# A Householder tridiagonalisation on one core: the next column from the reflected product, with the reflection's factor computed ahead of the product

## The reference

```python
L = jnp.diag(deg) - A
L_norm = d_inv_sqrt[:, None] * L * d_inv_sqrt[None, :]
_, U = jnp.linalg.eigh(L_norm)
agg = jnp.einsum('mn,bnd->bmd', U.T, features)
h = jax.nn.relu(agg @ W1 + b1)
out = h @ W2 + b2
return jnp.einsum('nm,bmd->bnd', U, out)
```

## Time and profile before

| | |
|---|---|
| median of 3 runs | 7619.89 us (7603.49 to 7624.76) |
| profiled execution | 7623.76 us, span 7622.0 us |
| mean granted TensorE clock | 0.811 |
| busy in the span: PE, DVE, ACT, POOL | 65%, 58%, 20%, 11% |
| the tridiagonal stage | 42 to 1437 us |

### The profile page before, as it was taken

How to read it: one execution, slowest core, us unless ns; L and a number is a source line. 1 busy time by engine, 2 the same in 40 slices (tenths; PEclk the granted TensorE clock), 3 DMA queues, 4 the chain that set the end, 5 groups by cost and what they waited for, 6 DMA issues and landing times. The chain is left out here.

```text
span 7622.0 us, 81119 instructions
## 1 busy us (share of the span) xinstructions
PE 4954.3 (65%) x22112; PEld 3479.5 (46%) x22112; DVE 4404.4 (58%) x17933; ACT 1555.7 (20%) x3409; POOL 852.4 (11%) x653
## 2 busy tenths in 40 slices
PE   5666544332003799740079967777697997977999
PEld 5666433210002577520069933333376443646676
DVE  5555666798995333348988866666633223343332
ACT  1111111243001244420000000000043532442333
POOL 0000000001000000000000068888400000000000
PEclk9999999975556799865555578888798997888799
DMA  0000000000000000010000000000000000000000
GB/s 24 1 1 1 1 1 1 1 1 1 1 1 1 12 0 0 2 12 21 0 0 0 0 4 4 4 4 4 3 0 13 0 0 7 0 3 12 1 0 22
DMA packets 72449, 30.60 MB, mean 4 GB/s; under 512 B 46714, under 2 KB 67860, under 8 KB 71956
## 3 DMA queue, kind: packets, MB, share of 16 engines
q1 hardware_dynamic: 52756, 23.65, 1.4%
q0 software_dynamic: 19456, 4.40, 0.9%
HBM read 22.89 MB, written 5.11 MB: 4 GB/s over the span
## 5 line engine op out<-in xcount | busy, mean ns | idle before, releaser
L1274 PE MATMUL l1f_ga_acc<-l1f_gas_prod,l1f_gas_ohl 128*128 128x512 f32 (+1 forms) x1824 | 778.8, 580 | 261.8 <-DVE l1f_gas_prod L1233 174.2
L1161 PE MATMUL l1f_gap_hist<-l1f_gap_ohh,l1f_gap_ohl 128*128 128x64 bf16 x4096 | 539.9, 308 | 361.4 <-DVE l1f_gap_ohh L1145 360.6
L1161 PEld LDWEIGHTS l1f_gap_hist<-l1f_gap_ohh,l1f_gap_ohl 128*128 128x128 bf16 x4096 | 492.8, 149 | 408.4 <-DVE l1f_gap_ohh L1145 400.7
L1274 PEld LDWEIGHTS l1f_ga_acc<-l1f_gas_prod,l1f_gas_ohl 128*128 128x128 f32 x1824 | 359.0, 208 | 681.7 <-issue 425.1
L1249 POOL DMA_INDIRECT l1f_gas_rs<-l1f_ga_table_s,l1f_gas_sidx x304 | 405.6, 1334 | 1016.0 <-DVE l1f_gas_didx L1205 923.6
L1683 PE MATMUL l0g_tri_dots<-l0g_tri_Z 128*128 128x7 f32 (+31 forms) x762 | 208.1, 394 | 462.2 <-DVE l0g_tri_Z L1850 448.5
L1233 DVE TENSOR_TENSOR l1f_gas_prod<-l1f_gas_ohh,l1f_gas_msg 128x1280 f32<-128x1280 f32 x304 | 454.2, 1494 | 10.4
L1249 POOL DMA_INDIRECT l1f_gas_rd<-l1f_ga_table_d,l1f_gas_didx x304 | 416.7, 1371 | 101.5 <-issue 101.5
L1260 ACT ACTIVATE l1f_gas_ex<-l1f_gas_ex 128x32 f32<-128x32 f32 x38 | 8.7, 229 | 2003.8 <-DVEq L1214 1896.2
L1683 PEld LDWEIGHTS l0g_tri_dots<-l0g_tri_Z 128*128 128x128 f32 x762 | 181.4, 318 | 479.6 <-DVE l0g_tri_Z L1848 462.5
L1143 DVE TENSOR_TENSOR l1f_gap_ohl<-l1f_gap_rep,l1f_gae_dlow 128x2048 bf16<-128x2048 bf16 x256 | 314.0, 1226 | 73.1 <-PE l1f_gap_hist L1161 72.6
(11 more groups left out here) (842 smaller groups left out, 10054.4 us busy)
## 6 DMA issues: line engine op xcount, KB each, us to landing
l1f_gas_rs<-l1f_ga_table_s,l1f_gas_sidx POOLq DMA_INDIRECT x304
l1f_gas_rd<-l1f_ga_table_d,l1f_gas_didx POOLq DMA_INDIRECT x304
out_dram<-top_x SPq DMA_DIRECT2D x2, 2048.0 KB, 12.2
l1f_gae_src<-in_L_ffn_edge_index_dram SPq DMA_DIRECT2D x1, 2048.0 KB, 7.3
l1f_gae_dst<-in_L_ffn_edge_index_dram SPq DMA_DIRECT2D x1, 2048.0 KB, 11.8
l2f_w<-in_L_ffn_expert_w_dram SPq DMA_DIRECT2D x3, 384.0 KB
l0f_l0f_W<-in_L_ffn_W_dram SPq DMA_DIRECT2D x1, 1024.0 KB
l1f_l1f_W<-in_L_ffn_W_dram SPq DMA_DIRECT2D x2, 512.0 KB
```

Of the source, the lines that this page charges most:

```text
L1161: last = nc.tensor.matmul(hist[:, :], ohl[:, j, :, c], ohh[:, j, :, c], start=False, stop=False)
L1274: last = nc.tensor.matmul(acc[:, c0 * T:c1 * T], ohl[:, c % 2, :], prod[:, c % 2, c0:c1, :].rearrange("p c t -> p (c t)"), start=False, st ...
```

## The change

The new column is written as (A x) and v alone: base = ya[0] * KV (+ a term for a vanishing column) and x' = vm * late[0] + base, where KV and vm = v * knk now carry the sign and the factor. `nk` is 1 / (root * ax + ns), with ns the squared norm, instead of the clamped sum t2, t3; a column whose squared norm is under 1e-30 gets a flag in ZF, and the flag also replaces the clamp when the vectors are kept. The whole block from ns to vm stands ahead of `ya[0]`; `late[1]` is used for KK only. The copies into VV move from ACT to DVE (`keep_vectors`). TensorE's wait for `w_set` comes after the wait for `applied` and still ahead of every matmul of the step. Its late matmuls wait for `ya_set` and `v_set`, which the instructions themselves raise.

```diff
                     pe.wait_ge(x_set, i + 1)
-                    pe.wait_ge(w_set, i)
                     if J == 0 and i > 0:
                         pe.wait_ge(applied, strip_of(i))
+                    pe.wait_ge(w_set, i)
...
-                    pe.wait_ge(late_in, i + 1)
+                    pe.wait_ge(ya_set, i + 1)
+                    pe.wait_ge(v_set, i + 1)
...
                     act.wait_ge(nk_set, i + 1)
+                    nc.scalar.activation(w["nkh"], w["nk"], ACT.Square, scale=0.5 ** 0.5).then_inc(act_step, 1)
+                    act.wait_ge(y_set, i + 1)
                     nc.scalar.activation(yn[:, h0:], y[:, h0:], ACT.Copy, scale=w["nk"]).then_inc(act_step, 1)
-                    nc.scalar.activation(w["nkh"], w["nk"], ACT.Square, scale=0.5 ** 0.5).then_inc(act_step, 1)
...
+                def keep_vectors(i, k, b):
+                    n = i + 1 - k * STRIP
+                    link(ts(moved[:, 0:n], ZF[:, k * STRIP:i + 1], -1.0, 1.0, ALU.mult, ALU.add))
+                    for h, top in ((0, min(n, P - 1 - k * STRIP)), (1, n)):
+                        if top > 0:
+                            link.free(tt(VV[:, h, k * STRIP:k * STRIP + top], Z[:, b, h, 1:2 * top:2], moved[:, 0:top], ALU.mult))
+                    dve.wait_ge(dve_step, link.n)
+                def current_times_x(i, J, h0, r, corr_at):
+                    dve.wait_ge(prod_done, i + 1)
+                    if J > 0:
+                        dve.wait_ge(dve_step, corr_at)
+                        ins = tt(ya[:, h0:, r, 0], prod[:, h0:HALF], corr[:, h0:], ALU.add)
+                    else:
+                        ins = nc.vector.tensor_copy(ya[:, h0:, r, 0], prod[:, h0:HALF])
+                    ins.then_inc(ya_set, 1)
...
+                    link.free(ts(ZF[:, at], dots[:, 0:1], 1e-30, None, ALU.is_lt))
                     dve.wait_ge(own_done, i + 1)
                     link.free(ts(w["sgn"], own[:, 0:1], 0.0, 2.0, ALU.is_ge, ALU.mult))
-                    link.free(ts(w["al2"], own[:, 0:1], 2.0, None, ALU.mult))
...
+                    link.free(stt(w["ax"], w["sgn"], -1.0, own[:, 0:1], ALU.add, ALU.mult))
+                    link.free(stt(w["ns"], ZF[:, at], 1e30, dots[:, 0:1], ALU.mult, ALU.add))
+                    link.free(stt(NB[:, at], w["sgn"], -1.0, w["root"], ALU.add, ALU.mult))
+                    dve.wait_ge(dve_step, ns_at)
+                    link.free(ts(w["den"], w["root"], w["ax"], w["ns"], ALU.mult, ALU.add))
+                    dve.wait_ge(dve_step, nb_at)
+                    stt(v, eye[:, h0:, r], NB[:, at], x, ALU.mult, ALU.add).then_inc(v_set, 1)
                     link.free(tt(V1[:, at], own[:, 0:1], NB[:, at], ALU.add))
+                    dve.wait_ge(dve_step, den_at)
                     if i > 0:
                         dve.wait_ge(act_step, 2 * i)
-                    link(nc.vector.reciprocal(w["nk"], w["t3"]))
+                    nc.vector.reciprocal(w["nk"], w["den"]).then_inc(nk_set, 1)
+                    link.free(stt(still[:, h0:], ya[:, h0:, r, 1], ZF[:, at], below[:, h0:, r], ALU.mult, ALU.mult))
+                    dve.wait_ge(nk_set, i + 1)
+                    dve.wait_ge(dve_step, v1_at)
+                    link.free(stt(KV[:, at], w["nk"], -1.0, V1[:, at], ALU.mult, ALU.mult))
+                    dve.wait_ge(dve_step, kv_at)
+                    link.free(stt(w["knk"], KV[:, at], -1.0, w["nk"], ALU.mult, ALU.mult))
+                    dve.wait_ge(dve_step, link.n)
+                    dve.wait_ge(v_set, i + 1)
+                    link.free(stt(vm[:, h0:], v, w["knk"], below[:, h0:, r], ALU.mult, ALU.mult))
+                    current_times_x(i, J, h0, r, corr_at)
+                    dve.wait_ge(ya_set, i + 1)
+                    stt(y[:, h0:], ya[:, h0:, r, 1], NB[:, at], ya[:, h0:, r, 0], ALU.mult, ALU.add).then_inc(y_set, 1)
+                    dve.wait_ge(dve_step, kv_at)
+                    link.free(stt(base[:, h0:], ya[:, h0:, r, 0], KV[:, at], below[:, h0:, r], ALU.mult, ALU.mult))
+                    dve.wait_ge(dve_step, base_at)
+                    link.free(tt(base[:, h0:], base[:, h0:], still[:, h0:], ALU.add))
                     dve.wait_ge(dve_step, link.n)
                     dve.wait_ge(late_done, i + 1)
+                    stt(Z[:, nb_next, h0:, 0], vm[:, h0:], late[:, 0:1], base[:, h0:], ALU.mult, ALU.add).then_inc(x_set, 1)
                     link.free(tt(w["c1"], late[:, 1:2], NB[:, at], ALU.mult))
+                    dve.wait_ge(dve_step, link.n)
                     dve.wait_ge(act_step, 2 * (i + 1))
                     link.free(ts(KK[:, at], late[:, 0:1], w["c1"], w["nkh"], ALU.add, ALU.mult))
-                    stt(Z[:, nb_next, h0:, 0], vnm[:, h0:], w["g"], base[:, h0:], ALU.mult, ALU.add).then_inc(x_set, 1)
+                    dve.wait_ge(dve_step, link.n)
+                    stt(wv, v, KK[:, at], yn[:, h0:], ALU.mult, ALU.subtract).then_inc(w_set, 1)
```

More of the change, by code:

```diff
@@ L1629, in tridiagonalise @@
         base = s.sb("base", [P, HALF])
-        vnm = s.sb("vnm", [P, HALF])
+        still = s.sb("still", [P, HALF])
+        vm = s.sb("vm", [P, HALF])
         NB = s.sb("NB", [P, N])
@@ L1635, in tridiagonalise @@
         VA = s.sb("VA", [P, N])
+        ZF = s.sb("ZF", [P, N])
+        moved = s.sb("moved", [P, STRIP])
         pick = s.sb("pick", [P, HALF, N])
-        names = ["sgn", "al2", "root", "t1", "t2", "t3", "nk", "nkh", "kb", "c1", "g1", "g"]
+        names = ["sgn", "ax", "ns", "root", "den", "nk", "nkh", "knk", "c1"]
         row = s.sb("row", [P, len(names)])
@@ L1647, in tridiagonalise @@
         diag_row = s.ps("diag_row", [P, N])
[L1648 to L1652, removed]
+        (masks, zeroed, init, dve_step, act_step, x_set, w_set, dots_done, own_done, prod_done, root_done, ya_set, v_set, nk_set,
+         y_set, late_done, va_kept, swapped, turned_done, turned_kept, rank_done, applied, picked, diag_done) = s.sems(
+            "masks", "zeroed", "init", "dve_step", "act_step", "x_set", "w_set", "dots_done", "own_done", "prod_done", "root_done",
+            "ya_set", "v_set", "nk_set", "y_set", "late_done", "va_kept", "swapped", "turned_done", "turned_kept", "rank_done",
+            "applied", "picked", "diag_done")
         def halves(i):
@@ L1685, in _ @@
                     last.then_inc(dots_done, 1)
-                    nc.tensor.matmul(own[:, 0:1 + 2 * J], eye[:, h1, r:r + 1].to_broadcast([P, P]), Z[:, b, h1, 0:1 + 2 * J],
-                                     start=True, stop=True).then_inc(own_done, 1)
+                    last = nc.tensor.matmul(own[:, 0:1 + 2 * J], eye[:, h1, r:r + 1].to_broadcast([P, P]), Z[:, b, h1, 0:1 + 2 * J],
+                                            start=True, stop=True)
+                    last.then_inc(own_done, 1)
                     for m in hs:
                         for h in hs:
-                            last = nc.tensor.matmul(prod[:, m:m + 1], As[:, h, bass.ts(m, P)], Z[:, b, h, 0:1],
-                                                    start=(h == hs[0]), stop=(h == 1))
+                            last = nc.tensor.matmul(prod[:, m:m + 1], As[:, h, bass.ts(m, P)], Z[:, b, h, 0:1], start=(h == hs[0]),
+                                                    stop=(h == 1))
                     last.then_inc(prod_done, 1)
-                    pe.wait_ge(late_in, i + 1)
+                    pe.wait_ge(ya_set, i + 1)
+                    pe.wait_ge(v_set, i + 1)
                     if i > 0:
@@ L1798, in _ @@
                     dve.wait_ge(dve_step, sgn_at)
[L1799 to L1802, removed]
-                    link.free(tt(V1[:, at], own[:, 0:1], NB[:, at], ALU.add))
[L1804 to L1809, removed]
@@ L1822, in _ @@
+                    link.free(stt(still[:, h0:], ya[:, h0:, r, 1], ZF[:, at], below[:, h0:, r], ALU.mult, ALU.mult))
+                    still_at = link.n
+                    dve.wait_ge(nk_set, i + 1)
+                    dve.wait_ge(dve_step, v1_at)
+                    link.free(stt(KV[:, at], w["nk"], -1.0, V1[:, at], ALU.mult, ALU.mult))
                     kv_at = link.n
[L1823 removed]
                     dve.wait_ge(dve_step, kv_at)
[L1825 removed]
+                    link.free(stt(w["knk"], KV[:, at], -1.0, w["nk"], ALU.mult, ALU.mult))
@@ L1826, in _ @@
                     base_at = link.n
-                    link.free(ts(w["kb"], KV[:, at], NB[:, at], 1.0, ALU.mult, ALU.add))
                     dve.wait_ge(dve_step, base_at)
-                    link.free(tt(base[:, h0:], base[:, h0:], below[:, h0:, r], ALU.mult))
+                    link.free(tt(base[:, h0:], base[:, h0:], still[:, h0:], ALU.add))
                     dve.wait_ge(dve_step, link.n)
                     dve.wait_ge(late_done, i + 1)
-                    link.free(tt(w["g1"], late[:, 1:2], w["kb"], ALU.mult))
@@ L1833, in _ @@
-                    g1_at = link.n
+                    if J == STRIP - 1 and k > 0:
```

(5 more changed lines are left out.)

32 lines of the change are left out of this document (7 added, 25 removed).

## The result

The changed kernel takes 7571.55 us (median of 5 runs, 7569.98 to 7582.9) against 7615.63 us for the kernel before in the same comparison: ratio 0.9946, 95% interval 0.9931 to 0.9961, that is 41 us less (30 to 53 by the interval; the two medians lie 44 apart). The forecast was 7565. A second comparison of the same kernel gave 7559.61 us and 0.9919 (0.9902 to 0.9935). The profiled execution took 7582.9 us. The head of its page and its table of stretches come first; the columns are those of the earlier trace rows. The last step on both blocks now ends at 780, and the stage at 1379 instead of 1440 us, so the second row holds some 11 us of what follows it.

A forecast was written before the change was run, and what follows sets the result against it. No engine is full; each tridiagonal step is a chain of latencies. From the 7620 us median, -44 (first half) and -14 (second half) give -58, plus 3 for stalls: 7565 us, range 7535 to 7606.

The forecast's parts named there:

- First half, front: TensorE's block to ya, 127 steps on both 128-row blocks: ya late by 0.03 to 0.34 us, middle 0.19.
- Second half, front: TensorE's block to ya, 127 steps on one block: 2.71 us instead of 1.86, 0.85 later.
- Tail: From ya to TensorE's next block: 2.30 us against 2.84 in the first half, 1.86 against 2.82 in the second.
- (c): ya_set sent by the instruction, not the queue: TensorE may start 0.03 us earlier or later, 8 us either way.
- (a): New column's pointer scalar in PSUM: 0 taken; other end 0.07 us each, +18 us over 254 steps.
- (b): VectorE instruction-stream stalls newly exposed in the first half: +3 us taken, between -5 and +11.
- (d): Extra waits before KV, vm, ya and late matmuls: 0 taken; other end 0.12 us each, +0.48 a second-half step.
- rival 1: Extra waits cost queue time, 0.12 us each before KV, vm, ya, y, late matmuls: +94 us, 7718; chance 6%.
- Rival 3: Second half gains nothing, front and tail nearly equal; only the first half pays, -44 us, 7579; chance 20%.

The follow-up runs named there:

- waits_swapped: The changed kernel with only the order of side-by-side waits swapped, the one that ends last written first, on TensorE and VectorE; stage 1308.6 us, ratio 0.9873.
- before_folded: The kernel before, old formula and order, with two semaphores raised by the instructions instead of VectorE's queue; stage 1345.1 us, ratio 0.9913.
- after_unfolded: The changed kernel with ya_set and nk_set sent by VectorE's queue again, formula and order kept; stage 1386.2 us, ratio 0.9979.
- ya_mid_c1: The changed kernel with ya right behind still, VectorE's other instructions dealt out around waits, and c1 ahead of the new column; stage 1199.5 us, ratio 0.9752.

## Why the prediction was right

The forecast was 7565, 55 us under the median that it started from, with the first half's wait for prod gone and the tail shorter in both halves. Step by step, by the views above.

- *First half, front:* block to `ya` 3.52 forecast, 584.32 - 580.81 = 3.51 measured. ns to `ya` 1.31 against 584.32 - 583.03 = 1.29. Over the whole half the mean of block to `ya` is 3.37, which is the 3.18 + 0.19 of the forecast. The steps were forecast from 5.5 to 5.8 us and are 5.51, 5.66 and 5.83 near a strip's start, middle and end.
- *Second half, front:* 2.71 forecast, 2.73 measured; L1812 to `ya` 1.61 (1.6).
- *Tail:* 1.86 forecast, 1.88 measured, but by two errors that cancel. `ya` to late was put at 0.27 from the queue's semaphore and is 0.21: bound (c), 0.03 either way, was too narrow. Late's end to Z was put at 0.04 and is 0.11: a wait that ends last and is written second, shown by waits_swapped. That they cancel is luck, and so is that the first half's tail comes out at 2.31 for 2.30.
- *(a), the pointer scalar in PSUM:* 0 taken. Z lasts 0.22 to 0.23 (mean 0.226 of 254), against a mean of 0.221 for L1867 with its pointer in SBUF and 0.213 for Z in the kernel before, and starts 0.04 after late in waits_swapped. The Trainium skill's 120 cycles against 58 for a PSUM source ("VectorE: DVE Perf Modes", TRN2 errata) would have lengthened it by 0.065 us; no run here shows that.
- *(b), stalls:* +3 taken, about -1 measured. Against undisturbed steps at the same place in a strip, the second half's mean step is 0.03 us longer (4.60 against 4.57) and in the kernel before was 0.05 longer (4.73 against 4.68). The first half's is 0.03 longer where it had been some 0.01: there they did come out from behind the wait for prod. That is some 7 us in all, against 8.
- *What the stalls are:* the prediction set them beside blocks of 256 instructions and found the two to agree. They don't. Leaving out a strip's first and last step and the wait for prod, the 14 traces have 344 places where VectorE starts an instruction 0.09 to 0.39 us later than it usually does behind the one in front, and in each they lie a multiple of 128 entries of VectorE's queue apart, within one or two, semaphore instructions counted. The kernel before has 32 entries a step in the second half, so one falls in every fourth step; the changed kernel has 31, so they wander. The kernels profiled twice have them in the same 28 steps both times. That they are instruction refills, no run shows.
- *(d), extra waits:* 0 taken, 0.12 at each the other end, rival 1 (its 7718 is 7714 by its own terms, or 7717 with (b)). KV follows the reciprocal at 0.19, knk follows KV at 0.20, vm 0.19, `ya` 0.14: satisfied waits cost nothing. The rival fell. What the prediction had not separated is which of two waits ends last, and in which order they are written.
- *Strip ends:* the step across a strip's end went from 11.06 to 10.90 us on two blocks and from 7.39 to 7.29 on one, about what the steps beside it gained (0.20 and 0.11; one of the three on two blocks has a stall and took 11.16). The first step of a new strip on two blocks gained more, 6.35 to 5.51, about 1 us in all beyond the others, and why stays open. The copies into VV that VectorE took over cost nothing that shows, as forecast.
- *Sum:* the first half gained 44.6 us against the 44 forecast, the second 16.7 against 14; the stage 61 against 58. Rival 3, no gain in the second half, gave 7579; the stage decides against it, the total (7571.55) lies between the two and would not have.
- *The total:* 41 us in the first comparison, 62 in the second (intervals 30 to 53 and 49 to 75). The prediction took the code outside the stage as constant; the profiled pair shows it moving by up to 20 us, half of it in `l2f_g`, which was granted a lower clock in one execution than in the other. So the 61 us of the stage are well measured, and whether the total falls by 41 or 62 is decided outside it.

The mechanism behind the sum was not wholly the one that I named. I priced the new chain from waits without a queue semaphore, and so had the folding in my sum without naming it: before_folded shows that it alone is worth 59 us, after_unfolded that the new formula and order without it are worth 18. They don't add up to 61 (59 + 18), because the semaphores cost less in the new order, 44 us: in the kernel before each lies on VectorE's path with 0.12, in the one after that of `ya` delays only TensorE's start, by 0.06.

That TensorE's block waits for w had no cost as the change made it, since before it waited there too; but the wait was itself worth 50 us of stage in ya_mid_c1, where the product ends last ahead of `ya`, shown by one matmul in the gap ahead of the wait. On the changed kernel, where `ya` waits for VectorE instead, that matmul was not tried.

## What to carry to other kernels

Where a step is a chain of small instructions, first list start to next start, and look for waits that nothing needs, semaphore instructions in the busy queue and instructions that follow the one whose result they read; here what such edits gave was twice to eight times (34 to 143 us) what the new formula and its order brought. Of several waits in front of an instruction, write the one that ends last first. And when a reordering moves work from the tail to the front, ask at once which of the moved instructions the front's result doesn't need: `ya` did not need the factor block (50 to 91 us).

## What the runs showed of the hardware

- A semaphore instruction in VectorE's queue behind a wait delays the next VectorE instruction by 0.12 us (0.32 against 0.20 start to start); raised by the instruction itself it costs nothing that shows.
- Two waits in front of an instruction: the one that ends last costs 0.06 to 0.07 us if it is the second, on VectorE (0.11 against 0.04) and on TensorE (0.34 against 0.27), and nothing if it is the first. The second one is a semaphore instruction of its own in the trace, the first is not.
- VectorE loses 0.09 to 0.39 us at places a multiple of 128 entries of its queue apart, where no other wait hides it; two traces of one kernel have them in the same steps.
- The same kernel was granted a mean clock of 0.515 and of 0.581 over the 352 matmuls of one stage in two executions, and that stage took 117.2 and 105.4 us. A difference of two profiled spans holds such parts; the stage that the change touches repeats within 1 us.
